# New orders of all engines behind the attention steps of a fused attention and mixture-of-experts layer

## What is computed

```python
sa, ca, ga, sb, cb, gb = split(silu(c) @ wmod)            # per batch; ga and gb kept away from 0
h = layernorm(x) * (1 + ca) + sa
x1 = x + ga * attention(h)       # 16 heads of 8, q and k normalised, softmax over 256 keys, gated, @ Wo + bo
h2 = layernorm(x1) * (1 + cb) + sb
p, experts = top_2(softmax(h2 @ router_w.T))              # 32 experts
y[token] = sum over its 2 experts e of p_e * (h2[token] @ W[e])
out = x1 + gb * y
```

## Time and profile before

| what | us |
|---|---|
| median of 3 runs | 967.23 |
| lowest and highest run | 966.6, 971.69 |
| span of the profiled execution | 977.1 |
| mean granted TensorE clock, share of full | 0.886 |

### The profile page before, as it was taken

The page is one execution under the profiler, slowest core; times in us unless marked ns, Lnnn a source line. Parts: engine busy times, 40 slices in busy tenths (PEclk is TensorE's granted clock), DMA queues, the critical chain, the costliest instruction groups (busy, mean ns, idle before and its releaser), DMA issues.

```text
span 977.1 us, 23375 instructions
## 1 busy us (share of the span) xinstructions
PE 751.6 (77%) x6334; PEld 512.0 (52%) x6334; DVE 676.2 (69%) x2015; ACT 564.5 (58%) x1300; POOL 507.0 (52%) x846
## 2 busy tenths in 40 slices
PE   4668988988888889998889788887988762524765
PEld 1234655545554566665666555564655551514665
DVE  4757878878786878788888687788876252611556
ACT  3156877776775778877778676676666522512100
POOL 5112455566654555555556666676665535273253
PEclk8579999999997999999999999999898765766888
DMA  2555545466444567767566666665554433754632
GB/s 66 146 146 142 117 115 148 120 150 151 123 115 122 152 168 183 179 175 181 158 179 177 178 161 172 162 167 152 152 154 122 128 108 86 211 154 133 183 81 81
DMA packets 178001, 141.70 MB, mean 145 GB/s; under 512 B 19540, under 2 KB 162612, under 8 KB 177876
## 3 DMA queue, kind: packets, MB, share of 16 engines
q1 hardware_dynamic: 122804, 99.54, 39.8%
q10 hardware_dynamic: 47392, 24.92, 8.8%
q0 software_dynamic: 7680, 15.74, 5.8%
HBM read 81.77 MB, written 57.80 MB: 143 GB/s over the span
## 4 chain that ended last, share of the span: by engine, by line
PE 39%; DVE 15%; issue 14%; DMA 9%; another core or an unknown queue 9%; SPq 7%; ACT 5%; POOL 1%; ACTq 0%; DVEq 0%; POOLq 0%
PE mx_ps L1937 10%; PE st_ps L1972 7%; PE o_ps L1986 6%; DVE negmax L1397 5%; DMA k_aug<-k_d 4%; DMA k_d<-parts 4%; PE st_ps L2132 3%; SPq L650 2%; PE misc L1995 2%; PE misc L1910 2%; SPq L602 2%; ACT pr L1089 2%; PE st_ps L2117 1%; PE misc L2029 1%
## 5 line engine op out<-in xcount | busy, mean ns | idle before, releaser
L1397 DVE TENSOR_REDUCE negmax<-mx_ps 128x2 f32<-128x512 f32 x512 | 339.0, 686 | 123.4 <-PE mx_ps L1937 68.1
L1089 ACT ACTIVATE pr<-st_ps 128x512 f32<-128x512 f32 x512 | 285.2, 599 | 77.9 <-PE st_ps L1972 71.9
L1937 PE MATMUL mx_ps<-k_aug,q_aug 126*128 126x256 bf16 x1024 | 200.1, 287 | 68.0 <-DVE negmax L1397 26.0
L1972 PE MATMUL st_ps<-q_aug,k_aug 128*128 128x256 bf16 x1024 | 190.5, 285 | 0.8 <-ACT ys_sb L1151 0.3
L1986 PE MATMUL o_ps<-pr,v_aug 128*32 128x256 f32 x2048 | 145.7, 404 | 37.4 <-issue 31.4
L921 POOL DMA_INDIRECT yg<-ys_d,gidx x120 | 117.7, 981 | 95.6 <-DVE yb L1627 42.0
L1937 PEld LDWEIGHTS mx_ps<-k_aug,q_aug 126*128 126x128 bf16 x1024 | 84.3, 100 | 158.3 <-issue 148.2
L906 POOL DMA_INDIRECT xs_d<-h,slot x120 | 120.5, 1004 | 59.2 <-DVE slot L1500 33.9
L1972 PEld LDWEIGHTS st_ps<-q_aug,k_aug 128*128 128x128 bf16 x1024 | 101.4, 105 | 30.1 <-issue 11.1
L1986 PEld LDWEIGHTS o_ps<-pr,v_aug 128*32 128x32 f32 x2048 | 57.3, 112 | 89.2 <-issue 69.5
L1095 ACT ACTIVATE oT<-o_ps 128x256 f32<-128x256 f32 x128 | 49.2, 384 | 77.7 <-remote 43.3
(11 more groups left out here) (192 smaller groups left out, 1280.3 us busy)
## 6 DMA issues: line engine op xcount, KB each, us to landing
xs_sb<-xs_d SPq DMA_DIRECT2D x248, 64.0 KB
ys_d<-ys_sb ACTq DMA_DIRECT2D x62, 256.0 KB
q_aug<-q_d SPq DMA_DIRECT2D x64, 192.0 KB
mod_o<-mod_d SPq DMA_DIRECT2D x32, 256.0 KB
bias_p<-bias_d SPq DMA_DIRECT2D x32, 200.0 KB
q_d<-parts SPq DMA_DIRECT2D x32, 192.0 KB, 2.1
k_d<-parts SPq DMA_DIRECT2D x32, 192.0 KB, 2.5
k_aug<-k_d SPq DMA_DIRECT2D x64, 96.0 KB
```

What stands on the lines that cost most here:

```text
L1089: nc.scalar.activation(pr[:, h % PR], st_ps[score_bank(b, h)][:], ACT.Exp, scale=SCALE).then_inc(exp_d, 1)
L1397: v.tensor_reduce(negmax[:, :, h], mx_ps[h % 2][:], AX.X, ALU.max, negate=True).then_inc(mx_d, 1)
L1937: last = t_.matmul(mx_ps[h % 2][:, qc], q_aug[b.par][0:MROW, h, qc * P:(qc + 1) * P], k_aug[b.par][0:MROW, h, :], start=True, stop=True)
L1972: last = t_.matmul(st_ps[score_bank(b, h)][:, kc], k_aug[b.par][:, h, kc * P:(kc + 1) * P], q_aug[b.par][:, h, :], start=True, stop=True)
```

## The change

The attention steps stay as they are. What changes in steps 35 to 39 and behind them:

- Drain steps have two groups instead of three. 14 groups (48 to 61) are left behind the steps instead of 9, and the first dense quarter stands in turn 4, behind all of them. Chunk 2 (batches 16 to 23) now ends a step later, so 14 batches are combined in the steps' part and 16 (14 to 29) behind.
- The orders within a drain step are new. DVE: router weights and expert choice first, then the denominators, the gated output and h2, then ranks and slot; combinations only at the ends of steps 35 and 36, those of batches 11 to 13 behind the steps. PE: the chain of batches 31 and 30 ahead of the second group. ACT: the router's exponential first. POOL: in step 35 two gathers ahead of the scatters.
- For batches 14 to 29, x1 rows and gate rows no longer go to the four buffers. They are loaded into `pr`, `qkvg` and `qn`, which are idle once the heads are done, by ACT's queue, in four bunches of four batches (`late_loads`): the first in step 37, the others in ACT's loop over the groups. DVE writes the result in place, so it waits for no store, and SP stores from there, behind all its loads of groups.
- h2 of batches 30 and 31 goes to a buffer of its own (`h2d`, over `sq`), so that it waits for no scatter.

```diff
-PS, PD = 2, 3
+PS, PD = 2, 2
-DENSE_FROM = 40
-QTURN = 1
+QTURN = 4
...
-        for _ in range(1 if s < DRAIN else 2):
+        for _ in range(0 if s == STEPS - 1 else 1):
...
+LATE = NS - COMBINED
+LATE_BUNCH = 4
...
+        def h2_of(b):
+            return h2[:, b.par] if b.n < NS else h2d[:, dense_of(b)]
+        def late_rows(n):
+            return pr[:].rearrange("p a t k -> p (a t k)")[:, (n - COMBINED) * TB * P:(n - COMBINED + 1) * TB * P].rearrange(
+                "p (t f) -> p t f", f=P)
...
             # SyncE
+            def drain_step(s, ahead, b0, b1, b2, b3, b4, b5, b6, b7, b8):
+                load_x_out(b4)
+                load_groups(s + 1)
+                for n in combined_in(s):
+                    final_loads(n)
+                store_x1(b4)
+                for n in combined_in(s - 2):
+                    final_store(n)
...
-            unsaved = [*combined_in(STEPS - 2), *combined_in(STEPS - 1)]
-            for i in range(-1, TURNS + FB):
-                turn(i, unsaved)
-                for group in BEHIND[XB + 2 * (i + 1):XB + 2 * (i + 2)]:
-                    load_group(*group)
+            for group in BEHIND:
+                load_group(*group)
+            for d in range(DENSE):
+                dense_loads(d)
+            for n in (*combined_in(STEPS - 2), *combined_in(STEPS - 1), *range(COMBINED, NS)):
+                final_store(n)
...
             # GpSimd
                 if s == DRAIN:
                     scatter(b7, 3)
+                    gather_in(s, 0, 1)
                 for k in range(TOPK * TB):
                     scatter(b6, k)
-                gather_in(s, 0, 1, 2, 3)
+                gather_in(s, *((2, 3) if s == DRAIN else range(TOPK * TB)))
...
             # ScalarE
+            def late_loads(j):
+                if j == 0:
+                    act.wait_ge(pv_d, GROUPS * NB)
+                    act.wait_ge(v_d, NB)
+                    act.wait_ge(qkT_ps, NB)
+                for n in range(COMBINED + LATE_BUNCH * j, min(COMBINED + LATE_BUNCH * (j + 1), NS)):
+                    act.wait_ge(x1_st[n % 2], 16 * (n // 2 + 1))
+                    act.dma_start(late_rows(n), x1_d[n].rearrange("(p t) f -> p t f", t=TB)).then_inc(late_ld[j], 16)
+                    act.dma_start(late_gate(n), mod_d[n, GB * P:(GB + 1) * P].partition_broadcast(P)).then_inc(late_ld[j], 16)
...
                 ln2_normalise(b5)
-                group_in(s, 0)
                 if s == DRAIN:
                     group_back(s - 1, 1)
                     group_stored(s - 1, 1)
+                router_exp(b7)
+                group_in(s, 0)
                 on_transposed(b4)
...
-                if s == DRAIN + 1:
+                if s == DRAIN + 2:
                     selectors()
+                    late_loads(0)
                 weights_turned(b8)
...
                 store_group(chunk, g, local)
+                if i % 3 == 0 and 0 < LATE_BUNCH * (i // 3 + 1) < LATE:
+                    late_loads(i // 3 + 1)
...
             # VectorE: combine
+                late = b >= COMBINED
+                x1_b = late_rows(b) if late else x1_f[:, i]
+                gate = late_gate(b) if late else gb_f[:, i]
...
-                wait(dve, out_st[i], 16 * (b // FB))
-                v.tensor_tensor(of[:, i], yb[:], x1_f[:, i], ALU.add).then_inc(of_d, 1)
+                if not late:
+                    wait(dve, out_st[i], 16 * (b // FB))
+                v.tensor_tensor(x1_b if late else of[:, i], yb[:], x1_b, ALU.add).then_inc(of_d, 1)
...
             # VectorE: drain step, new order
+                router_sum(b8)
+                router_inverse(b8)
+                keep_weights(b8)
+                scale_wo(b4)
+                top_logits(b6)
+                top_experts(b6)
+                one_hot(b6)
+                chosen(b6)
                 for qc in range(TB):
                     denominator(b4, qc)
                 factor(b4)
                 for qc in range(TB):
                     gated_out(b4, qc)
+                table_out(s)
                 scale_ln2(b5)
                 shift_ln2(b5)
                 ranks(b6)
                 add_counts(b6)
                 chosen_ranks(b6)
                 slot_number(b6)
+                x_plus_bias(b4)
+                less_largest(b6)
                 residual(b4)
...
-                combine_in(s - 1, 1)
-                quarter_in(s, 2)
+                if s <= DRAIN + 1:
+                    combine_in(s - 1, 0)
...
             # TensorE: drain step, new order
                 transpose_out(b4, 1)
                 expert_rows(s, 0)
+                count_before(b6)
+                table_turned(s)
                 transpose_on(b4)
+                if s == DRAIN:
+                    expert_out(s, 0)
+                    transpose_h2(b5)
+                else:
+                    transpose_h2(b5)
+                    expert_out(s, 0)
+                project_out(b4)
+                logits(b5)
                 expert_rows(s, 1)
                 expert_out(s, 1)
                 turn_weights(b8)
```

More of the change, by code:

```diff
@@ L149, in combined_in @@
     return COMBINED_IN.get(s, [])
-def quarters_of(s):
-    lo = 3 * (s - DENSE_FROM)
-    return [u for u in range(lo, lo + 3) if 0 <= u < DENSE * QS]
-FIRST_BEHIND = min(max(3 * (STEPS - DENSE_FROM), 0), DENSE * QS)
 TURN_GROUPS, TURN_QUARTERS = 3, 1
@@ L169, in quarters_at @@
 def quarters_at(i):
-    lo = FIRST_BEHIND + TURN_QUARTERS * (i - QTURN)
-    return [u for u in range(lo, lo + TURN_QUARTERS) if FIRST_BEHIND <= u < DENSE * QS]
+    lo = TURN_QUARTERS * (i - QTURN)
+    return [u for u in range(lo, lo + TURN_QUARTERS) if 0 <= u < DENSE * QS]
 def combined_at(i):
@@ L451, in build @@
         f_ld = [sem(f"f_ld{i}") for i in range(FB)]
+        late_ld = [sem(f"late_ld{i}") for i in range(-(-LATE // LATE_BUNCH))]
         mix_d, of_d = sem("mix_d"), sem("of_d")
@@ L677, in final_store, with attention_step @@
                 sp.wait_ge(of_d, b + 1)
-                sp.dma_start(out[b].rearrange("(p t) f -> p t f", t=TB), of[:, b % FB]).then_inc(out_st[b % FB], 16)
-            def step(s, ahead, b0, b1, b2, b3, b4, b5, b6, b7, b8):
+                sp.dma_start(out[b].rearrange("(p t) f -> p t f", t=TB),
+                             of[:, b % FB] if b < COMBINED else late_rows(b)).then_inc(out_st[b % FB], 16)
+            def attention_step(s, ahead, b0, b1, b2, b3, b4, b5, b6, b7, b8):
                 if s == 0:
@@ L1601, in dense @@
                 quarter(u)
-            def quarter_in(s, i):
-                if i < len(quarters_of(s)):
-                    dense(quarters_of(s)[i])
             def combine_in(s, i):
@@ L1616, in combine @@
                 wait(dve, yg_ld[i], 64 * (b // FB + 1))
-                wait(dve, f_ld[i], 32 * (b // FB + 1))
+                late = b >= COMBINED
+                x1_b = late_rows(b) if late else x1_f[:, i]
+                gate = late_gate(b) if late else gb_f[:, i]
+                if late:
+                    j = (b - COMBINED) // LATE_BUNCH
+                    dve.wait_ge(late_ld[j], 32 * min(LATE_BUNCH, LATE - LATE_BUNCH * j))
+                else:
+                    wait(dve, f_ld[i], 32 * (b // FB + 1))
                 for t in range(TB):
@@ L1717, in shift_ln2 @@
                 wait(dve, h2a_d, b.n + 1)
-                wait(dve, scat[b.par], 64 * min(b.nth, (NS + 1 - b.par) // 2))
-                wait(dve, h2T_ps, b.n - 1)
+                if b.n < NS:
+                    wait(dve, scat[b.par], 64 * b.nth)
+                    wait(dve, h2T_ps, b.n - 1)
+                else:
+                    dve.wait_ge(ss_d, NB)
                 dve.wait_ge(h2_d, b.n)
-                v.tensor_tensor(h2[:, b.par], h2a[:], mod_o[:, b.par, 2:3, :].broadcast_to([P, TB, P]), ALU.add).then_inc(h2_d, 1)
+                v.tensor_tensor(h2_of(b), h2a[:], mod_o[:, b.par, 2:3, :].broadcast_to([P, TB, P]), ALU.add).then_inc(h2_d, 1)
             @of_batch
@@ L1849, in turn @@
                     combine(combined_at(i))
-            for at in (STEPS - 1,):
-                for n in combined_in(at):
-                    combine(n)
+            for at in range(DRAIN + 1, STEPS):
+                combine_in(at, 0)
             for i in range(TURNS):
@@ L2019, in transpose_h2 @@
                 for t in range(TB):
-                    last = t_.transpose(bank[:, t * P:(t + 1) * P], h2[:, b.par, t], ident[:])
+                    last = t_.transpose(bank[:, t * P:(t + 1) * P], h2_of(b)[:, t], ident[:])
                 last.then_inc(h2T_ps, 1)
@@ L2090, in quarter @@
                     last.then_inc(yd_ps, 1)
-            def quarter_in(s, i):
-                if i < len(quarters_of(s)):
-                    quarter(quarters_of(s)[i])
             def table_turned(s):
```

70 lines of the change are left out of this document (23 added, 47 removed).

## The result

The changed kernel takes 981.55 us (median of 4 runs, 976.69 to 990.52) against 969.46 for the kernel before in 4 runs beside it: ratio 1.0135, 95% interval 1.009 to 1.018. It is slower; the forecast was 963.7, and the result lies above its range of 944 to 979. The profiled execution took 990.52, the longest of the four: a span of 988.5 and 2.0 around it. (In the kernel before, the steps of the engines that the rows name begin at SP L680, POOL L930 and L958, ACT L1173 and L1218, DVE L1632 and L1787, PE L2149 and L2207.)

The account below looks back on a forecast made before the run. It took the tail to be bound by gather bursts that hold other engines, then by expert groups, dense quarters and gathers. Landmark shifts moved the end from 977.1 to 973.6, -3.5 us, so 967.2 became 963.7; range 944 to 979.

Parts of the forecast that it names:

- Steps 1 and 2: First drain step and first gather burst: batch 29's slot at 791.0, 3.4 us earlier; table copy at 818.1.
- Step 3: From the first burst's end to gather 16, which needs group 47 stored: 34.4 us, gather 16 at 852.5.
- two more groups, 4.6 worse: Slow bound on the stretch up to gather 16: two more groups there make it 4.6 us worse.
- Step 4: Second burst, gathers 16 to 21, stays and ends its hold 2.35 us earlier; VectorE's 28.5 us wait credited nothing.
- the hold: Stretch around a long gather burst where other engines stand; begins about 4 us in, ends 1 to 4 us behind.
- Step 5: Ten expert groups left after the second burst at 2.6 us each: 26 us, quarter 0 at 912.9 against 909.78.
- Step 6: Quarter 0 to gather 22, through VectorE's quarter and combination 18: 5.2 us, gather 22 at 918.1.
- Step 7: Seven turns from gather 22 to 29, one quarter and one combination each, 6.26 us: 43.8 us, gather 29 at 961.9.
- Step 8: From gather 29 to the end, with one combination behind the last gather: 11.7 us, end at 973.6.
- the 916.4: Break-even start of quarter 0 in us; the prediction called itself wrong if quarter 0 came beyond it.
- groups are starved: Slower rival: SyncE stands at batch 11's store, twelve groups left at 3.24 us, quarter 0 about 921; 976; chance 0.22.
- The lock-out of GpSimd: Slower rival: VectorE locks GpSimd out, 28 gathers from 15 on 0.42 us longer each, 12 us; 975 to 976; chance 0.04.

Follow-up runs that it names:

- E3: Changed kernel with the second group's rows turned and copied ahead of the first group's result on TensorE and ScalarE; ratio 1.0175 to the kernel before.
- E11: Changed kernel with three groups a step from step 35 on and the second group's rows ahead of the first one's result; ratio 1.015 to the kernel before.
- E1: Changed kernel with its 32 late loads issued by SyncE in place of ScalarE; ratio 1.0128 to the kernel before.
- E13: Changed kernel with the late loads on SyncE, run again in the short condition; ratio 1.011 to the kernel before.
- E10: Changed kernel with its first dense quarter in turn 7 in place of turn 4; ratio 1.012 to the kernel before.
- E4: Changed kernel with its first dense quarter in turn 1 in place of turn 4; ratio 1.0043 to the kernel before.
- E5: The changed kernel run again unchanged, in the short condition; ratio 1.025 to the kernel before.
- E2: Changed kernel with the stores of combinations 11 and 12 behind SyncE's loads of the groups behind the steps; ratio 1.0069 to the kernel before.
- E16: Changed kernel: three groups a step, quarter 0 in turn 7, stores 11 and 12 moved, combinations 11 to 13 in steps, late loads on SyncE; ratio 0.991.
- E6: Changed kernel with gathers 17 to 21 held on GpSimd until the last group is copied; ratio 1.052 to the kernel before.
- E7: Changed kernel with gathers 16 to 21 let go in pairs, one pair for each group copied from 48 on; ratio 1.025 to the kernel before.

## Why the prediction was wrong

- **Steps 1 and 2** held: slot at 791.79 (said 791.0), table copy at 818.28 (818.1).
- **Step 3** failed, and this is the first error: gather 16 at 859.77, not 852.5. It took a group at 2.3 us, the pace of the earlier trace rows, where the change puts the second group's rows behind the first one's result. ScalarE's results then come 3.1 to 4.3 us apart (847.62, 851.88, 855.00) and wait 2.34 us for TensorE, which had waited for ScalarE. VectorE's last step ends late too, by the 6.73 us for TensorE's turned weights at 847.93. The bound of "two more groups, 4.6 worse" did not hold 7.3. E3's trace shows the part in this condition: with the overlap back, gather 16 is 8.9 us earlier. In the short one E11, three groups a step and overlap, brings it 3.6 us forward and the last group 6.9. The 4.3 us for the late loads in step 37 lay beside the selectors (L1154, 3.6 us) and were over-charged.
- **Step 4** held in its length (33.6 us from gather 16 to the first group behind the hold, 34.4 said) and in its warning: VectorE's wait moved to quarter 0.
- **Step 5** failed in size: ten groups were left, as said, but they took 29.7 us (3.0 each) in place of 26 (2.6). It counted the late loads that moved to ScalarE as a relief of SyncE, without counting them here on the queue that they moved to; two bunches stand in this stretch, 4.70 and 4.51 us ahead of the rows' copy. E1 prices the late loads at 3.2 us of the last group in this condition (123.9 against 127.1 us behind the last scatter), E13 at 6 in the short one.
- **Step 6** held for the distance (4.7, said 5.2) but did not see what it stands for. The sum runs through quarter 0 and so has the wait in it; but "This is what the later quarter costs" is said of 5.2 us, where GpSimd stands idle for 38. E10 closes that hole in the short condition, where it is 17.4 us, and returns 0.013; in the long one E4 returns 0.009.
- **Step 7**: 48.7 us, said 43.8. The gathers do not come singly 6.3 us apart: three times two batches go in a row (22 and 23, 25 and 26, 27 and 28), and at the end of each of these rows of eight gathers VectorE's quarter waits 2.2 to 3.3 us for TensorE or a releaser that is not named, as here. In E5 the same seven batches take 37.9 us.

```profile
937.76 0.69 DVE L1618 TENSOR_TENSOR q_aug<-misc,h2Td 128x512 f32<-128x512 f32 x1 [2.88 <-remote]
```

- **Step 8** held: 12.0, said 11.7.

The terms sum to the miss: 7.3 - 0.8 + 3.7 at quarter 0, -0.5, +4.9 and +0.3 make 14.9, from 973.6 to 988.5; the medians miss by 15.6 (3.5 under the kernel before was said, 12.1 over it came). Quarter 0 at 923.07 is past the 916.4 that the prediction named as a sign of being wrong.

The rival "groups are starved", 976 and decided from quarter 0 at 921, came nearest in time and was given 0.22, in part by luck: it had gather 16 on time and twelve groups behind the hold at 3.24, and the trace has ten at 3.0, while 7.3 of the 10.2 us that quarter 0 is late arise before gather 16. Its reason, SyncE's stores, is a part of the loss by E2; E3 (in its trace) and E11 show another part in the order of the groups on TensorE and ScalarE, and E13 one in the late loads.

The lock-out of GpSimd, the rule of the Trainium skill ("SBUF — State Buffer", "SBUF: two separate sides"), did not come: with combinations 11 to 28 beside them the gathers of batches 15 to 29 last

```profile
L941 POOL DMA_INDIRECT yg<-ys_d,gidx x60: 947/952/1177, 851.2 to 980.4; - x60
```

so at most 0.23 us over the median. No row tells in which mode VectorE's operations ran. (The rival's price took 28 of these 60 gathers.) What the trace could not tell and the prediction leaned on was the hold: E5 shows that the same kernel can run without it.

The change as such was not wrong. Its parts (chain of the last batches first, late rows into idle buffers), with three groups a step, the late loads on SyncE, the stores of combinations 11 and 12 behind the loads of groups, combinations 11 to 13 in their steps and the dense quarters where gather 22 does not wait for them, beat the kernel before by 0.9% (E16).

## What to carry to other kernels

Behind a loop, write the end as the later of its serial chains and keep both in view: list what each item of a chain waits for and what stands ahead of that in the other engine's order; a hole in the later chain comes out at the end, as far as the other chain does not end later; a hole in the other one does not. When work moves to another queue, charge it there as well, at its own duration, inside the chain that this queue carries. Before two items of a step are put one behind the other, count how often the two engines hand them over: overlapped items went at 2.3 us here, serial ones at 3.1 to 4.3.

## What the runs showed of the hardware

The same program with the same 24 gathers in 33 us keeps TensorE at 11.58 us of work and the DMA engines at 0.44 in the long condition (the window of the changed kernel above); in the short one it is, over the window that answers to it,

```profile
760.00:793.00 33.00, 20.96 (x107) 19.65 (x107) 5.54 (x16) 10.29 (x18) 22.82 (x24) 0.71 0.89 254
```

254 GB/s against 122, with GpSimd's own pace unchanged at 1.26 us a gather. So in these windows the pace of the indirect DMAs does not feel what holds the others, and a comparison of two orders can come out at 1.4% or at 2.5% by the condition. What makes the hold was not found. Not tried: E6 and E7 in the long condition, and a profile of the two conditions with the neighbours' traffic.
